# The first microseconds of a wide attention layer: order of norm, weight halving, subtractions and first scores

## The reference

```python
def _L0_xattn_ref(x_norm, ctx, mask, position_bias, Wq, Wk, Wv, Wo):
    q, k, v = x_norm @ Wq.T, ctx @ Wk.T, ctx @ Wv.T      # 16 heads of 64
    scores = q @ k.T / 8 + position_bias                  # -inf where mask
    return softmax(scores) @ v @ Wo.T
x = x + _L0_xattn_ref(_layernorm(x), ctx_1024, mask, ...)
```

## Time and profile before

| | before |
|---|---|
| runs | 1499.92, 1505.87, 1507.51 us |
| median | 1505.87 us |
| profiled execution | 1497.63 us, its span 1495.7 us |
| granted TensorE clock, mean | 0.953 |
| TensorE busy | 1357.8 us, 91% |
| VectorE busy | 1038.6 us, 69% |
| ScalarE busy | 888.9 us, 59% |
| GpSimd busy | 820.1 us, 55% |

### The profile page before, as it was taken

One profiled execution on the slowest core, in us unless ns is written; L12 is line 12 of the kernel. 1 busy time (PEld: TensorE's weight loads), 2 busy tenths in 40 slices (PEclk: granted clock), 3 DMA queues, 4 the chain that ended last, 5 costly groups with the idle time before them and its releaser, 6 DMA issues.

```text
span 1495.7 us, 37017 instructions
## 1 busy us (share of the span) xinstructions
PE 1357.8 (91%) x14494; PEld 838.4 (56%) x14494; DVE 1038.6 (69%) x2508; ACT 888.9 (59%) x1471; POOL 820.1 (55%) x778
## 2 busy tenths in 40 slices
PE   4799999998979999999978899987978897999988
PEld 3365666665757777777733344433666565444446
DVE  5788888888744344443758989875798476677764
ACT  4487777774759999999834444432233332555542
POOL 6488878776658899989844243212353002434310
PEclk9799999999989999999979999986989899899998
DMA  8000000000013210001101201000000000000000
GB/s 273 5 9 9 9 9 9 2 2 16 30 33 98 61 45 14 28 28 46 33 5 32 65 33 33 30 1 28 1 3 10 0 1 4 5 9 9 2 1 29
DMA packets 25796, 39.62 MB, mean 26 GB/s; under 512 B 7028, under 2 KB 13080, under 8 KB 25144
## 3 DMA queue, kind: packets, MB, share of 16 engines
q1 hardware_dynamic: 25080, 35.58, 7.4%
q0 software_dynamic: 576, 2.10, 0.7%
HBM read 38.72 MB, written 1.05 MB: 27 GB/s over the span
## 4 chain that ended last, share of the span: by engine, by line
PE 67%; DVE 19%; issue 5%; POOL 5%; ACT 3%; DMA 1%; SPq 0%; POOLq 0%; DVEq 0%; ACTq 0%
PE bank L1765 10%; PE bank L1706 10%; PE bank L695 5%; DVE sbuf L834 4%; PE bank L633 4%; PE bank L2231 3%; PE bank L1164 2%; PE bank L649 2%; PE bank L1989 2%; PE bank L1268 2%; POOL sbuf L1118 2%; PE bank L2210 2%; DVE sbuf L851 2%; PE bank L1196 2%; POOL sbuf L1112 2%
## 5 line engine op out<-in xcount | busy, mean ns | idle before, releaser
L1716 ACT ACTIVATE sbuf<-bank,sbuf 128x512 f32<-128x512 f32 (+1 forms) x512 | 323.1, 684 | 30.1 <-PE bank L1706 18.1
L1736 POOL TENSOR_TENSOR sbuf<-sbuf 128x512 f16<-128x512 f32 x256 | 304.9, 1199 | 56.1 <-ACT sbuf L1716 55.1
L310 POOL TENSOR_TENSOR sbuf<-sbuf 128x2 f32<-128x2 f32 (+1 forms) x48 | 39.7, 827 | 353.8 <-DVE sbuf L305 353.8
L1765 PEld LDWEIGHTS bank<-sbuf 128*128 128x128 f16 x3072 | 194.3, 98 | 67.3 <-issue 7.7
L1765 PE MATMUL bank<-sbuf 128*128 128x128 f16 x3072 | 214.6, 220 | 6.3 <-DVEq L1853 6.3
L1706 PE MATMUL bank<-sbuf 128*128 128x512 f16 x768 | 209.2, 382 | 0.0
L834 DVE TENSOR_REDUCE sbuf<-bank 128x4 f32<-128x1024 f32 x128 | 156.3, 1221 | 64.4 <-PE bank L649 51.5
L1848 DVE SCALAR_TENSOR_TENSOR sbuf<-bank,sbuf 128x128 f32<-128x128 f32 x256 | 71.7, 341 | 165.1 <-PE bank L1765 164.9
L1118 POOL TENSOR_TENSOR sbuf<-sbuf 128x512 f16<-128x512 f32 x128 | 148.2, 1179 | 56.8 <-ACT sbuf L1361 56.7
L695 PE MATMUL bank<-sbuf 128*32 128x256 f32 x2048 | 140.3, 393 | 1.6 <-ACT sbuf L782 1.6
L1112 POOL TENSOR_TENSOR sbuf<-sbuf 128x512 f16<-128x512 f32 x96 | 112.0, 1185 | 27.4 <-ACT sbuf L1349 27.1
(11 more groups left out here) (294 smaller groups left out, 2726.8 us busy)
## 6 DMA issues: line engine op xcount, KB each, us to landing
sbuf<-w SPq DMA_DIRECT2D x32, 256.0 KB, 2.9
sbuf<-bias_t SPq DMA_DIRECT2D x4, 1024.0 KB, 11.7
sbuf<-ctx_t SPq DMA_DIRECT2D x24, 128.0 KB, 3.4
sbuf<-bias_q POOLq DMA_DIRECT2D x4, 512.0 KB, 11.6
sbuf<-mask_t SPq DMA_DIRECT2D x8, 256.0 KB, 2.7
sbuf<-bias_t SPq DMA_DIRECT2D x8, 256.0 KB, 3.0
sbuf<-mask_q SPq DMA_DIRECT2D x8, 256.0 KB, 3.7
sbuf<-bias_q SPq DMA_DIRECT2D x8, 256.0 KB, 4.4
```

The source lines that it names most:

```text
L1716: last = act.activation(to, bank[u % 4][:, :], ACT.Gelu, bias=b1[u // U][:, u % FT0:u % FT0 + 1], scale=1 / SCALE)
L1736: g.tensor_tensor(hid16[1][:, u % BUFS, :], hid[:, u % 4, :], hid16[0][:, u % BUFS, :], ALU.subtract)\
L1765: last = pe.matmul(bank[4 + out_no % 2][:, j * P:(j + 1) * P], hid16[h][:, u % BUFS, j * P:(j + 1) * P], w2_16[p][:, w, f * D:(f + 1) * D] ...
```

## The change

- The turns of the norm's quarters go to banks 4, 7, 2 and 3 instead of 0 to 3 (`TURNS`), so banks 0 and 1 are free for scores.
- GpSimd: the powers of quarters 2 and 3 stand after subtractions 1 and 2, and the second batch's context after all 12 subtractions.
- VectorE: `eye16` is copied behind the first statistics; the first halving stands after the first scale, the second after the scale of quarter 1, the third after the scale of quarter 2; then low parts 0 and 1, the last scale, low part 2, masks, the `drop` copy, key sums; low part 3 and the bias sum follow the first score's maxima.
- TensorE: the keys product and the first score stand before the last projection; the wait for all of `nrm_xt` stands before the units, not before the first score.

```diff
@@ -961,6 +961,7 @@
             EARLY_PAIRS = PAIRS - 2
             PROBS = 4
             S_BANK, W_BANK, O_BANK, PR_BANK, TR = (0, 1), (2, 3), 4, (5, 6), 7
+            TURNS = (O_BANK, TR) + W_BANK
             s_pair, w_pair = psum[:, 0:2 * HW], psum[:, 2 * HW:4 * HW]
 
             top[0] = phases
@@ -1095,8 +1096,6 @@
                         for at in range(DH0, VS):
                             last = g.memset(rest[:, :, :, at:at + 1], 1.0 if k == 0 and at == DH0 else 0.0)
                     last.then_inc(s["vready"], 1)
-                for k in range(1, CHUNKS):
-                    nm.power(g, 2 * k, 2 * k + 2)
 
                 def contexts(b):
                     g.wait_ge(ctx_in[b % 2], b // 2 * 16 + 16)
@@ -1118,10 +1117,12 @@
                         g.tensor_tensor(p_low[:, u % PROBS, cols], exps[:, u % 2, cols], p_high[:, u % PROBS, cols],
                                         ALU.subtract).then_inc(s["probs"], 1)
 
+                nm.power(g, 2, 4)
                 for k in range(JOBS):
                     split_(0, k)
-                    if k == 3:
-                        contexts(1)
+                    if k in (1, 2):
+                        nm.power(g, 2 * k + 2, 2 * k + 4)
+                contexts(1)
                 for u in range(UNITS):
                     b, n = divmod(u, NP)
                     jobs = JOBS_AT[n] if b + 1 < B else ()
@@ -1271,20 +1272,22 @@
                         last.then_inc(s["outed"], 1)
 
                 pe.wait_ge(eye_in, 16)
-                nm.turn(pe, 0, 2, bank[0])
+                nm.turn(pe, 0, 2, bank[TURNS[0]])
                 for k in range(JOBS):
                     project(0, k)
                     if k % 3 == 2 and k // 3 + 1 < CHUNKS:
                         c = k // 3 + 1
-                        nm.turn(pe, 2 * c, 2 * c + 2, bank[c])
-                pe.wait_ge(s["keys"], 1)
-                pe.matmul(bank[TR][:, 0:E0], ones, key2, start=True, stop=True).then_inc(s["keys"], 1)
-                pe.wait_ge(nrm_xt, nm.ready(B - 1))
-                pe.wait_ge(eyes_ready, 3)
-                for u in range(AHEAD):
+                        nm.turn(pe, 2 * c, 2 * c + 2, bank[TURNS[c]])
+                    if k == JOBS - 2:
+                        pe.wait_ge(s["keys"], 1)
+                        pe.matmul(bank[TR][:, 0:E0], ones, key2, start=True, stop=True).then_inc(s["keys"], 1)
+                        pe.wait_ge(eyes_ready, 3)
+                        scores(0)
+                for u in range(1, AHEAD):
                     scores(u)
                     if u == 1:
                         maxima(0)
+                pe.wait_ge(nrm_xt, nm.ready(B - 1))
                 for u in range(UNITS):
                     b, n = divmod(u, NP)
                     jobs = JOBS_AT[n] if b + 1 < B else ()
@@ -1327,13 +1330,13 @@
             def scalar(act):
                 act.wait_ge(eyes_ready, 1)
                 act.activation(warm, half[:, 0:8], ACT.Exp)
-                nm.copy(act, 0, 1, bank[0])
+                nm.copy(act, 0, 1, bank[TURNS[0]])
 
                 def high(a, z, src):
                     act.wait_ge(nrm_turned, z)
                     act.activation(x16[:, a:z, 0, :], src.rearrange("p (b s) -> p b s", s=S), ACT.Copy).then_inc(s["x_high"], 1)
 
-                high(1, 2, bank[0][:, S:2 * S])
+                high(1, 2, bank[TURNS[0]][:, S:2 * S])
 
                 def project(b, k):
                     act.wait_ge(s["projected"], b * JOBS + k + 1)
@@ -1371,7 +1374,7 @@
                     project(0, k)
                     if k % 3 == 2 and k // 3 + 1 < CHUNKS:
                         n = k // 3 + 1
-                        high(2 * n, 2 * n + 2, bank[n])
+                        high(2 * n, 2 * n + 2, bank[TURNS[n]])
                 maxima(0)
                 for u in range(UNITS):
                     b, n = divmod(u, NP)
@@ -1402,19 +1405,15 @@
                 c.step(v.memset(part_of[:, :, :, 2], -LIFT)).settle()
                 v.wait_ge(x_in[0], 16)
                 nm.stats(v, 0, 2)
-                nm.scale(v, 0, 2)
-                for k in range(1, CHUNKS):
-                    v.wait_ge(x_in[k], 16)
-                    nm.stats(v, 2 * k, 2 * k + 2)
-                    if k >= 2:
-                        nm.scale(v, 2 * k - 2, 2 * k)
+                v.wait_ge(eye_in, 16)
+                v.tensor_copy(eye16, eye).then_inc(eyes_ready, 1)
 
                 def low(k):
 
                     a, z = max(2 * k, 1), 2 * k + 2
                     v.wait_ge(s["x_high"], k + 1)
-                    src = bank[k][:, (a - 2 * k) * S:2 * S].rearrange("p (b s) -> p b s", s=S)
-                    v.tensor_tensor(x16[:, a:z, 1, :], src, x16[:, a:z, 0, :], ALU.subtract).then_inc(nrm_xt, z - a)
+                    of = bank[TURNS[k]][:, (a - 2 * k) * S:2 * S].rearrange("p (b s) -> p b s", s=S)
+                    v.tensor_tensor(x16[:, a:z, 1, :], of, x16[:, a:z, 0, :], ALU.subtract).then_inc(nrm_xt, z - a)
 
                 def halves(k):
                     w = (wq, wk0, wv)[k]
@@ -1423,16 +1422,18 @@
                     v.scalar_tensor_tensor(w16[k][:, 1, :], w, SCALE, w16[k][:, 0, :], ALU.mult, ALU.subtract)\
                      .then_inc(s["w16"], 1)
 
+                nm.scale(v, 0, 2)
+                halves(0)
+                for k in range(1, CHUNKS):
+                    v.wait_ge(x_in[k], 16)
+                    nm.stats(v, 2 * k, 2 * k + 2)
+                    if k >= 2:
+                        nm.scale(v, 2 * k - 2, 2 * k)
+                        halves(k - 1)
                 low(0)
+                low(1)
                 nm.scale(v, B - 2, B)
-                halves(0)
-                low(1)
-                halves(1)
                 low(2)
-                halves(2)
-                v.wait_ge(const_in, 16 * (2 + len(near)))
-                v.tensor_copy(drop, drop_col.unsqueeze(2).to_broadcast([P, 2 * HG, P])).then_inc(eyes_ready, 1)
-                v.tensor_copy(eye16, eye).then_inc(eyes_ready, 1)
 
                 def masks(b, k):
                     v.wait_ge(mask_in[b % 2], b // 2 * 32 + 32)
@@ -1492,13 +1493,16 @@
 
                 for k in range(2):
                     masks(0, k)
+                v.wait_ge(const_in, 16 * (2 + len(near)))
+                v.tensor_copy(drop, drop_col.unsqueeze(2).to_broadcast([P, 2 * HG, P])).then_inc(eyes_ready, 1)
                 v.scalar_tensor_tensor(g0, near["keys_t"], 2.0, near["rw_t"], ALU.mult, ALU.add)
                 v.scalar_tensor_tensor(key2, near["keys_t"], -1.0, near["keys_t"], ALU.mult, ALU.mult).then_inc(s["keys"], 1)
-                v.wait_ge(s["keys"], 2)
-                v.tensor_tensor(g0b, bank[TR][:, 0:E0], near["rb"], ALU.add)
-                low(CHUNKS - 1)
                 for u in range(AHEAD):
                     scores(u)
+                    if u == 0:
+                        low(CHUNKS - 1)
+                        v.wait_ge(s["keys"], 2)
+                        v.tensor_tensor(g0b, bank[TR][:, 0:E0], near["rb"], ALU.add)
                     if u == 1:
                         cut(0)
                 for u in range(UNITS):
```

## The result

| | before | with the change |
|---|---|---|
| median | 1504.76 us (13 runs, 1499.92 to 1507.51) | 1492.41 us (13 runs, 1486.07 to 1500.48) |
| ratio, 95% interval | | 0.9935, 0.9914 to 0.9956 |
| profiled execution | 1497.63 us, span 1495.7 | 1493.39 us, span 1491.3 |
| granted TensorE clock, mean | 0.953 | 0.953 |

The ratio is a gain of 9.8 us (6.6 to 12.9); the medians lie 12.35 apart. Forecast were 13 us and 1493. Measured again twice, beside the kernel before, the change gave 0.9937 (0.9914 to 0.9960) and 0.9949 (0.9932 to 0.9965). So it is faster by some 0.5 to 0.65%, 7.7 to 9.8 us, and the three intervals lie between 0.35 and 0.9%. The 12.35 between these two medians is at the high end: over all 77 runs of the kernel before the median is 1502.73, over the 30 of the change 1493.4.

What follows compares the result with a forecast made beforehand. Start-up bound by two chains, GpSimd's and VectorE's, with a lock between them; 10.5 us to the first score plus 3.7 from the high clock is 14.2, less 1.2 is 13: 1493 us off the 1505.87 median, range 1484 to 1503.

Steps and rivals of the forecast that it cites:

- First halving between loads: VectorE's idle time before x's second quarter: the halving costs 1.6 us, ends at 9.3, and is hidden.
- GpSimd: Reordered start-up: first subtraction after 11.4, last power ends at 20.8, subtraction 8 ends at 29.2 instead of 32.77.
- VectorE: Reordered start-up list: last scale ends at 28.2, the rest ahead of the first score at 30.7.
- the row's bad price: VectorE's last norm scale: 3.04 us, as the earlier trace shows for four scales beside GpSimd subtractions.
- TensorE to the first score: Last turn 0.5, projections 9 and 10 1.05 us each, key sums 0.6: first score at 31.5, 10.5 us sooner.
- From the first score to the first bias addition: 11.67 us before, all at the low clock; the high clock was to save 3.7 us.
- Score before projection 11 and the low part: Projection 11, low part and bias sum fit into waits between scores and maxima: cost nothing; in full, 2.0 us.
- The 1.2 us for missed waits: Taken off the 14.2 us gain for one more GpSimd instruction waited for that the schedule may miss.
- The shift stands to the end: After the first bias addition there are only waits among engines, so the whole gain lasts to the kernel's end.
- Rival 1: Low clock in the first scores: gain only 10.5 us, or 8.8 with slow projections; 1495 to 1497 us; chance 0.26.
- Rival 2: More GpSimd–VectorE lock, at scales, masks, copy and key sums: first score at 37 to 38, 1498 to 1501 us; chance 0.16.
- Rivals 3 and 4: 3: first score waits at old place, 1503 to 1505, chance 0.05; 4: low clock in 64-unit loop, slower, 0.03.

Runs made afterwards that it cites:

- the pause: The change with one wait more: GpSimd's subtraction 5 waits until VectorE's last norm scale is done; 1491.29 us (10 runs), ratio 0.9924 to the kernel before.
- The filled version: The change plus unread TensorE matmuls, two behind projection 8 and four behind the second score; 1486.50 us (4 runs), again 1489.19 us (6 runs).
- the change again: The change unaltered, measured on another chip; 1491.93 us (6 runs), ratio 0.9937 to the kernel before.
- the pause with filling: The change with GpSimd's subtraction 5 waiting for the last scale and four unread matmuls behind the second score; 1490.60 us (6 runs), ratio 0.9925.

## Why the prediction was right

- **First halving between loads: right**, hidden. It took 2.07 us and not 1.6. Most of that isn't GpSimd's: with GpSimd still, the parts take 0.69 and 1.22 us, 1.94 from start to end, so the 0.54 and 1.08 read from the earlier trace rows were too small. It ended 0.06 us before the next quarter's statistics, which no longer wait for the load: the margin was gone, at no cost.
- **GpSimd: right.** First subtraction at 12.62 (12.5 said), last power ends at 20.90 (20.8), subtraction 8 at 28.75 (29.2; the prediction's own terms, 20.8 and six times 1.13 and 1.0, give 28.6).
- **VectorE: right.** Last scale 23.82 to 27.65 (24.5 to 28.2 said), at the row's bad price of 3.04 plus a first wait of 0.7: 3.83 measured. That price is the lock, as the pause shows (1.10). Everything ahead of the first score was done at 30.14 (30.7).
- **TensorE to the first score: right in sum**, 31.80 against 31.5, by errors that cancel. The last turn came 0.6 us sooner and the key product cost 0.2 instead of 0.6, but the turn and projections 9 and 10 ran at the low clock: 1.11 and 3.13 us for 0.5 and 2.1. That the sum came out is luck.
- **From the first score to the first bias addition: the term that was mis-sized.** 3.7 us were forecast for the high clock (its parts, 2.2, 1.3 and 0.3, add up to 3.8), 1.7 came. The step that failed is "so I take the high clock": TensorE was dense from 27.7 to 33.7, and the clock did rise within that, at 31; but after the waits that followed (0.87 and 2.18 us) it was down again at 38, and with these waits filled it stayed up. The stretch from 27 to 28, with 0.09 us of work at 1.00, showed the clock of that moment, not one that stays: with the change the same microsecond has 0.85 and the next 0.50. The filled version bounds the term: held at 1.00 all the way it is 11.67 - 8.45 = 3.2 us.
- **Score before projection 11 and the low part: right to cost nothing.** With it undone the first score came 2.8 us later, 1.0 of it from the later scale; the 1.8 left are about the 2.0 put down for the three pieces.
- **The 1.2 us for missed waits: not found in this place.** The scale of quarter 1, beside the new early subtractions, took 1.94 us and not 1.11, that of quarter 2, beside a power, 1.32, and the times behind them still came as forecast. The sum of 14.2 was too high by 2.2 at the addition, through the clock, and the 1.2 taken off for another reason hid half of that.
- **The shift stands to the end: right up to 1155** (10.6 us), **and only roughly at the end.** The medians beside each other are 12.35 us apart, but the ratios give 9.8, 9.5 and 7.7 us, and the pair of profiles ends 4.4 apart. The prediction had "only waits among engines" behind the first addition; in fact the stages at 364 and 1155 ran longer by 2.5 and 6.6 us at a lower clock. That 1493 was hit has luck in it: the base of three runs, 1505.87, was about 3 us too high, and the 13 us about as much.

**Rival 1** (low clock in the first scores, 0.26) was half true: scores 0 and 1 ran fast, the third score and the weighing slow, and the clock was low in projections 9 and 10 too, after the wait that ended at 27.70 (it stayed up through the one near 15, where the rival had it fall). Its price, 8.8 to 10.5 us (with two projections at 1.77 us its low end should be 9.1), is as near to the gain at the end as the forecast's 13, so the time alone doesn't tell the two apart; the addition, at 41.75, lies between the forecast's 40 to 41 and the rival's 43 to 44. The Trainium skill's page "TensorE: Matmul & The Clock Gate", section "A second HAM failure mode: psum-queue depth-cycling", tells of a clock that swings between its two levels when TensorE idles for short times between groups of matmuls. The trace agrees as far as it goes: 0.50, 1.00 and 0.50 again between 28 and 41, with waits before both falls.

**Rival 2** had its lock in the scales (1.94 and 3.83), but not at the masks and the copy, where GpSimd was idle from 28.75 to 31.72; in the pause run, where it wasn't, they paid 3.0 us, just what the rival said. On the powers the row was the better guide than the Trainium skill's page "SBUF — State Buffer", section "Who interferes with whom", by which the scales would wait for the whole power: four scales beside one take 1.32 us, alone 1.10. The power sometimes pays instead: here it takes 1.75 us and ends with VectorE's next halving instruction, both at about 20.9, but in two later profiles with the same order (the change again, and the pause with filling) it takes 1.01. What decides that isn't known.

**Rivals 3 and 4** are out: nothing waited at its old place, and the clock is 1.00 from 43 on.

## What to carry to other kernels

When two engines wait for each other's whole instructions, read the short instructions on the critical one: four scales that take 1.10 us alone cost 3.83. But holding the other engine back moves its work next to whatever comes later: the pause gave the scales 2.7 us back, and the instructions behind them lost 3.0. Look at when the whole list ends. A start-up phase is a handful of chains that end within a microsecond of each other, so work through all of them; undoing one part of this change cost 2.9 to 4.5 us at the first addition, and none alone was the gain. And forecast the clock of a sparse phase as low unless something fills it: here six unread matmuls were worth 1.9 us at the first addition.

## What the runs showed of the hardware that was not expected

- Six subtractions beside a halving and the scales took 8.62 us in a row, 1.44 each, where two alone take 2.26. In exchange the four scales beside them lost 2.7 us, some 0.7 each.
- The first halving's two parts took 0.80 and 1.23 us beside GpSimd's issues and memsets, against 0.69 and 1.22 with GpSimd still: next to nothing, where subtractions made it 1.00 and 2.02.
- The clock fell after a wait of TensorE of 1.37 us (at 28) and after one of 2.18 (at 38), and stayed at 1.00 with 1.03 and 1.89 us of unread work in these waits, or with the first of them gone (the pause).
- A stage of 768 matmuls took 367.2 or 367.3 us where it started between 362.9 and 364.2, and 364.5 to 365.3 where it started earlier or later: a fall of the clock (0.74 against 1.00 from 384 to 388) that comes with when the code runs. A stage of 320 took between 91.9 and 98.8 us. So a pair of single profiles can mislead by several us, and the rows near the change say more about it than the end of the span.
